# Expert kernel on one core: order of ScalarE's and GpSimd's lists in the experts pass, wider weight pieces, and a key pass in which TensorE turns nothing

## The reference

```
h  = x + layernorm(rs * (attention(layernorm(x) Wq, ctx Wk, ctx Wv) Wo + bo)) * gamma + beta
n  = layernorm(h)                                  # 4096 rows
scores = softmax(n @ gate_weight.T)                # 64 experts
topk_w, topk_idx = top_k(scores, 8), weights normalised to sum 1
for each chosen pair (row, expert e):
    y[row] += w * ((silu(n @ w_gate[e]) * (n @ w_up[e])) @ w_down[e])   # inner width 384
out = h + y
```

## Time and profile before

| | |
|---|---|
| median of 3 runs | 6712.06 us (6709.46 to 6721.78) |
| profiled execution: its own time | 6714.65 us |
| its span, first to last instruction | 6713.0 us |
| granted TensorE clock, mean | 0.983 |
| projections | 12.4 to 1089 us |
| attention and output passes | to 2836 us |
| experts pass, TensorE | 2852.5 to 6695.6 us, 286 tiles |
| busy: PE, DVE, ACT, POOL | 6472.6, 3663.3, 2923.7, 2308.0 us |

### The profile page before, as it was taken

The page is one execution under the profiler, slowest core; times in us unless marked ns, Lnnn a source line. Parts: engine busy times, 40 slices in busy tenths (PEclk is TensorE's granted clock), DMA queues, the critical chain, the costliest instruction groups (busy, mean ns, idle before and its releaser), DMA issues.

```text
span 6713.0 us, 107844 instructions
## 1 busy us (share of the span) xinstructions
PE 6472.6 (96%) x32234; PEld 5731.1 (85%) x32235; DVE 3663.3 (55%) x4544; ACT 2923.7 (44%) x3606; POOL 2308.0 (34%) x2178
## 2 busy tenths in 40 slices
PE   9999999999999999699999999999999999999998
PEld 7888887887888788589989888899899999989987
DVE  4443324999999799744454454443533444444444
ACT  3321224888888655333343343332422333333333
POOL 1000000000000155544545454554444444545554
PEclk9999999999999999899999999999999999999999
DMA  8863555555555676456676676665655656666666
GB/s 258 232 196 143 155 146 144 127 128 127 128 132 130 174 173 171 110 152 160 163 212 162 164 188 160 163 164 111 186 111 111 139 137 164 146 155 164 161 158 149
DMA packets 873577, 1049.72 MB, mean 156 GB/s; under 512 B 440705, under 2 KB 670849, under 8 KB 873474
## 3 DMA queue, kind: packets, MB, share of 16 engines
q0 software_dynamic: 123984, 368.70, 24.0%
q1 hardware_dynamic: 593104, 382.50, 23.6%
q10 hardware_dynamic: 156386, 297.29, 13.2%
HBM read 725.85 MB, written 322.31 MB: 156 GB/s over the span
## 4 chain that ended last, share of the span: by engine, by line
PE 33%; DMA 8%; issue 6%; DVE 4%; POOL 3%; ACT 2%; ACTq 1%; SPq 0%; another core or an unknown queue 0%; POOLq 0%; DVEq 0%
DMA out<-moe_y,moe_rec_s 4%; PE moe_ps_gate L1374 4%; PE moe_ps_gate L1375 4%; PE moe_ps_gate L1376 4%; PE moe_ps_up L1376 4%; PE moe_ps_up L1374 4%; PE moe_ps_up L1375 4%; PE moe_ps_y L1363 3%; PE moe_ps_y L1362 3%; PE moe_ps_y L1361 3%; DMA moe_tokens<-h2st,moe_rows 3%; POOL moe_tokens L1325 2%; DVE moe_ps_turned L1477 1%; DVE moe_d_lo L1467 1%; DVE moe_gu_lo L1467 1%
## 5 line engine op out<-in xcount | busy, mean ns | idle before, releaser
L1325 POOL DMA_INDIRECT moe_tokens<-h2st,moe_rows x1156 | 1273.1, 1101 | 515.2 <-issue 265.7
L1374 PE MATMUL moe_ps_gate<-moe_gu_hi,moe_xT_hi 128*128 128x384 f32 x2288 | 811.3, 355 | 73.8 <-DVE moe_xT_lo L1471 53.9
L1414 ACT COPY moe_y<-moe_ps_y 128x1024 f32<-128x1024 f32 x287 | 291.2, 1015 | 1249.4 <-DMA out<-moe_y,moe_rec_s 1051.9
L1375 PE MATMUL moe_ps_gate<-moe_gu_lo,moe_xT_hi 128*128 128x384 f32 x2288 | 784.4, 343 | 0.0
L1376 PE MATMUL moe_ps_gate<-moe_gu_hi,moe_xT_lo 128*128 128x384 f32 x2288 | 783.4, 342 | 0.0
L1376 PE MATMUL moe_ps_up<-moe_gu_hi,moe_xT_lo 128*128 128x384 f32 x2288 | 764.3, 334 | 0.0
L1375 PE MATMUL moe_ps_up<-moe_gu_lo,moe_xT_hi 128*128 128x384 f32 x2288 | 764.2, 334 | 0.0
L1374 PE MATMUL moe_ps_up<-moe_gu_hi,moe_xT_hi 128*128 128x384 f32 x2288 | 764.2, 334 | 0.0
L1484 DVE SCALAR_TENSOR_TENSOR moe_hidden<-moe_silu,moe_rec_w,moe_ps_up 128x384 f32<-128x384 f32 x286 | 175.8, 615 | 1009.2 <-PE moe_ps_up L1376 694.4
L1361 PE MATMUL moe_ps_y<-moe_d_hi,moe_hT_hi 128*128 128x512 f32 x1722 | 673.5, 391 | 12.8 <-DVE moe_hT_lo L1491 10.3
L1363 PE MATMUL moe_ps_y<-moe_d_hi,moe_hT_lo 128*128 128x512 f32 x1722 | 677.1, 393 | 0.0
(11 more groups left out here) (202 smaller groups left out, 14047.6 us busy)
## 6 DMA issues: line engine op xcount, KB each, us to landing
first_raw<-in_w_gate ACTq DMA_DIRECT2D x63, 1536.0 KB, 7.7
first_raw<-in_w_up ACTq DMA_DIRECT2D x63, 1536.0 KB
moe_raw_d<-in_w_down ACTq DMA_DIRECT2D x63, 1536.0 KB
proj_a_raw<-in_ctxT POOLq DMA_DIRECT2D x64, 512.0 KB, 5.6
kst<-proj_o SPq DMA_DIRECT2D x256, 128.0 KB, 2.8
vst<-proj_o SPq DMA_DIRECT2D x64, 512.0 KB, 2.6
qst<-proj_o SPq DMA_DIRECT2D x256, 128.0 KB, 2.2
att_kt<-kst SPq DMA_DIRECT2D x64, 512.0 KB, 3.5
```

The source lines that it names most:

```text
L1325: nc.gpsimd.indirect_dma_start(out=tokens[:, g * (H // G):(g + 1) * (H // G)], out_offset=None, in_=h2_quarters, in_offset=bass.IndirectOf ...
L1374: nc.tensor.matmul(o[:, 0:I], xT_hi[:, c], gu_hi[:, b, k, c], start=(c == 0), stop=False)
L1375: nc.tensor.matmul(o[:, 0:I], xT_hi[:, c], gu_lo[:, b, k, c], start=False, stop=False)
```

## The change

In the projections pass the transposes by TensorE go, with `tps`, `xT`, their copies and the identity. SyncE stores the normalised rows `xn` as rows (`xnst`), with columns regrouped by quarter; for Q, GpSimd loads a block with four DMAs into `xg`, which reuses the space of `xin` and `xn`, VectorE turns it in four pieces with 32x32 transposes into `a_raw`, and the splits read and write it in the turned order. In the experts pass GpSimd's scatter comes ahead of its gathers, ScalarE's silu is made at the end of the tile before, gate and up are split in 4 pieces (128x1536), some of them placed between other steps, and the load of down moves from the end of an expert to the first tile of the next. TensorE still turns `hidden`.

```diff
+        xin, xn = rows[:, 0:2], rows[:, 2:4]
+        xg = rows[:].rearrange("p q n -> p (q n)").rearrange("p (g n) -> p g n", g=GROUPS)
...
+                    if p == Q:
+                        if not is_first(t2, b):
+                            pool.wait_ge(turned_done, PIECES * t)
+                        for k in range(P // W):
+                            part = xnst[bass.ds(t * HALF, HALF), k * (H * W // P):(k + 1) * (H * W // P)]
+                            pool.dma_start(xg[k * W:(k + 1) * W], part.rearrange("(g b) n -> b g n", b=W)).then_inc(xg_in, 16)
+                        return
...
+                def turn(p, t2, b, k):
+                    n = number(p, t2, b)
+                    dve.wait_ge(xg_in, 16 * (P // W) * (2 * t2 + b + 1))
+                    dve.wait_ge(a_lo_done, (n - 1) * PIECES + k + 1)
+                    columns_of_piece = slice(k * CP * W, (k + 1) * CP * W)
+                    nc.vector.transpose(a_raw[:, chunks(k)].rearrange("p c t -> p (c t)"), xg[:, :, columns_of_piece]).then_inc(turned_done, 1)
...
-                            for c in range(C):
-                                last = nc.tensor.transpose(tps[:, jb, c], xn[:, jb, c * P:(c + 1) * P], ident[:])
-                            last.then_inc(t_done, 1)
...
+        CHUNKS = C // 2
+        GU = 2 * C // CHUNKS
...
                 with pool.Fori(0, last_tile + 1) as t:
+                    add(t - 1)
                     gather(t + 3)
-                    add(t - 1)
...
-                def load_gate_up(e):
-                    act.wait_ge(w_lo_done, PIECES * (e - 1) + GU)
+                def load_gate_up(e, k):
+                    act.wait_ge(w_lo_done, PIECES * (e - 1) + (k + 1) * GU // 2)
...
+                def tile(t):
+                    tokens_high(t + 1)
+                    output(t - 1)
+                    turned_high(t)
+                    gated(t + 1)
+
+                def first_tile(t, e, b, more, is_first):
+                    tokens_high(t + 1)
+                    load_down(e)
+                    split(e, b, 0, 2)
+                    output(t - 1, is_first)
+                    split(e, b, 2, 3)
+                    turned_high(t)
+                    split(e, b, 3, GU)
+                    gated(t + 1)
                     if more:
-                        load_gate_up(e + 1)
+                        load_gate_up(e + 1, 0)
+                        load_gate_up(e + 1, 1)
...
                         split(e + 1, 1 - b, GU, PIECES)
-                        if has_second:
-                            load_down(e + 2)
...
                     tokens_low(t + 1)
+                    if e is not None:
+                        split(e, b, 0, 1)
                     turn_tokens(t + 2)
                     if e is not None:
-                        split(e, b, 0, GU)
+                        split(e, b, 1, 2)
+                    if e is not None:
+                        split(e, b, 2, 3)
                     dve.wait_ge(hT_hi_done, t + 1)
                     nc.vector.tensor_tensor(hT_lo[:], hT_ps, f32(hT_hi[:]), ALU.subtract).then_inc(hT_lo_done, 1)
+                    if e is not None:
+                        split(e, b, 3, GU)
```

More of the change, by code:

```diff
@@ L146, in stores_before @@
         def stores_before(p, t2, b, g):
-            return 16 * (sum(STORES[i] * NB * G // 2 for i in range(p)) + STORES[p] * ((2 * t2 + b) * (G // 2) + g // 2))
+            return 16 * (sum(STORES[i] * NB * ROUNDS // 2 for i in range(p)) + STORES[p] * ((2 * t2 + b) * (ROUNDS // 2) + g // 2))
         def piece(p, half, k):
@@ L163, in norm_tile, with turned, split @@
             return LN * (2 * t2 + b) + g // 2 if g % 2 == 0 else None
-        def transposed_tile(p, t2, b, g):
-            if g % 2 == 0 or p == Q or p == V and not (is_first(t2, b) and g == 1) or p == K and is_first(t2, b) and g == 1:
-                return None
-            if p == V:
-                return LN * NB - 1
-            return LN * (2 * t2 + b) + (g - 3) // 2
-        def stored_tiles(p, t2, b, g):
-            return LN // 2 * (NB if p == V else 2 * t2 + b) + (g - 3) // 2 // 2
+        def turned(p, k):
+            raw = a_raw[:, chunks(k)]
+            if p < Q:
+                return raw
+            return raw.rearrange("p c t -> p (c t)").rearrange("p (g c b) -> p c g b", g=GROUPS, b=W)
+        def split(p, tile, b, k):
+            piece = tile[:, b, chunks(k)]
+            if p < Q:
+                return piece
+            return piece.rearrange("p c (g b) -> p c g b", b=W)
         def chunks(k):
@@ L298, in root @@
                     nc.scalar.activation(std[:, jb], mv[:, jb, 1:2], ACT.Sqrt, bias=eps[:]).then_inc(std_done, 1)
-                def transposed(j, jb, tiles_before):
-                    act.wait_ge(t_done, j + 1)
-                    if not (known(tiles_before) and tiles_before == 0):
-                        act.wait_ge(xT_stored[jb], 16 * tiles_before)
-                    nc.scalar.copy(xT[:, jb], tps[:, jb]).then_inc(xT_done, 1)
                 for k in range(PIECES):
@@ L316, in body @@
                         weights_high(p, 1, 1)
-                    for g in range(G):
+                    for g in range(ROUNDS):
                         evacuate(p, t2, b, g)
@@ L386, in body @@
                         weights_low(p, 1, 1)
-                    for g in range(G):
+                    for g in range(ROUNDS):
+                        if after and after[0] == Q and g < PIECES:
+                            turn(*after, g)
                         evacuate(p, t2, b, g)
@@ L403, in body @@
                     n = number(p, t2, b)
-                    for g in range(G):
+                    for g in range(ROUNDS):
                         if not (p == K and is_first(t2, b) and g < BANKS):
-                            pe.wait_ge(o_lo_done, n * G + g - BANKS + 1)
+                            pe.wait_ge(o_lo_done, n * ROUNDS + g - BANKS + 1)
                         half, r = g // LN, g % LN
@@ L1371, in tile @@
                         for c in range(C):
-                            if e is not None and c % 2 == 0:
-                                pe.wait_ge(w_lo_done, PIECES * e + k * (C // 2) + c // 2 + 1)
+                            if e is not None and c % CHUNKS == 0:
+                                pe.wait_ge(w_lo_done, PIECES * e + (k * C + c) // CHUNKS + 1)
                             nc.tensor.matmul(o[:, 0:I], xT_hi[:, c], gu_hi[:, b, k, c], start=(c == 0), stop=False)
@@ L1426, in load_down, with gated @@
                     act.dma_start(raw_d[:], w_down[bass.ds(e, 1)].rearrange("o (c p) i -> p (o c) i", p=P)).then_inc(raw_in[2], 16)
-                def tile(t, e=None, b=None, more=False, is_first=False):
+                def gated(t):
                     act.wait_ge(gu_done, 2 * t + 1)
```

114 lines of the change are left out of this document (49 added, 65 removed).

## The result

The changed kernel takes 6838.17 us (median of 4 runs, 6830.48 to 6849.09) against 6711.95 for the kernel before: ratio 1.0186, 95% interval 1.0169 to 1.0204. It is 126 us slower, where 149 us less was predicted.

The account below looks back on a forecast made before the run. TensorE was taken as the bound, busy nearly all the time. Gains of 115 us in the experts pass, 29 in the key pass and 4.7 at the end, 149 off 6714.65, gave 6566, as median 6563 us; range 6520 to 6640.

Parts of the forecast that it names:

- Scatter ahead: Experts pass: scatter issued 5.4 us after up's product ends (U), landing before the next `y` needs it; cost 0.
- The cover is 3 us and more even with weights: Experts pass: later gathers still leave VectorE 3 us or more to turn tokens and make `hT_lo`; cost 0.
- Silu last: Experts pass, ScalarE: silu ahead of the down pieces, so no stall at an expert switch, with 0.7 us of cover.
- The 26 stalls: Experts pass: TensorE's waits for `hidden` and the tokens' low part, 4.6 us each; 21 at ordinary switches give 96 us.
- Pieces: Experts pass, VectorE: four wide pieces take 6.8 us, eight narrow about 7.0; the 0.2 us is off TensorE's path.
- One-tile experts: Experts pass: six experts with a single tile, 33 us of stalls after the change against 36 today; gain 3 us.
- the start: Start of the experts pass: two wide pieces instead of eight narrow ahead of `hT_lo`; gain 3.5 us.
- the tenths: Experts pass: 34 us of small losses in many periods without named cause; a third, 12 us, gained.
- Key pass: Projections: TensorE no longer turns 32 tiles at 0.91 us each; gain 29.0 us, lower end 24.
- The end: End of the experts pass: scatter of the last tile but one issued at 6690.3, everything after 4.7 us sooner.
- C: Experts pass: gathers become the bound, period 13.8 instead of 12.80, 286 us more, about 6850 us; chance 0.05.
- the waits of `moe_y` for the scatter near 0: Sign in the profile after that would show the prediction right: `y` copies hardly wait for the scatter.

Follow-up runs that it names:

- e2: The changed kernel with GpSimd's gathers ahead of its scatter again: 6735.09 us, ratio 1.0052 to the kernel before.
- e7: The changed kernel with the scatter's row numbers copied out, so SyncE loads the next record after that copy instead of the landing: 6806.44 us, ratio 1.0157.
- e11: e7 with SyncE loading the scatter's record a whole tile ahead: 6647.33 us, ratio 0.9905.
- e14: e9 with the scatter ahead of the gathers and its record loaded a tile ahead: 6903.23 us, ratio 1.0304.
- e3: The kernel before with only the scatter moved ahead of the gathers: 6883.19 us, ratio 1.0271.
- e8: e4 with the load of down moved into an expert's first tile: 6666.74 us, ratio 0.9954.
- e9: The changed kernel's projections pass with the experts pass of e8: 6659.80 us, ratio 0.9918.
- e4: The kernel before with only the silu moved to the end of ScalarE's list: 6783.95 us, ratio 1.0125.
- e12: e9 with four wide weight pieces in place of eight narrow ones: 6715.84 us, ratio 1.0007.
- e17: e11 with eight narrow weight pieces in the places of the four wide ones: 6626.34 us, ratio 0.9872.
- e16: e11 with `hT_hi` and `hT_lo` ahead of the third wide piece on ScalarE and VectorE: 6625.36 us, ratio 0.9869.
- e1: The kernel before with only the changed projections pass, its experts pass untouched: 6668.37 us, ratio 0.9954.
- e10: e5 with the loads of gate and up held until all four pieces are split: 6757.45 us, ratio 1.0076.
- e5: e2 with the turn ahead of VectorE's first weight piece: 6689.87 us, ratio 0.9986.
- e15: e14 with the load of gate let go once the gate pieces are split: 6901.69 us, ratio 1.0301.

## Why the prediction was wrong

*Scatter ahead* is the step that failed, in two places. The first: "It is issued when `y` is ready: U+5.4". The scatter needs three things: `y`, the landing of the one before, and its own row numbers. The prediction followed the first two. The third comes through SyncE, whose list is ordered for gathers ahead: there `rows_done` comes early in the tile, and the group records are fetched while `rec_s` waits for the scatter's landing anyhow. With the scatter ahead, `rows_done` comes behind it, and the record of the next scatter behind `rows_done`. The profile of before showed the cover: SyncE waited for `hidden` and for the scatter, and 19.9 us only for row numbers. Priced at 0, scatter ahead cost 90 us in the changed kernel (e2). e7 and e11 show that this is the record: moved a tile ahead it takes 169 us off e7 and 189 off after.

The second: "The cover is 3 us and more even with weights; cost 0". These 3 us are U+25.5 less the latest landing, U+20.6, less the turn and `hT_lo`. In a first tile two pieces, 3.4 us, stand between these two, so with weights on the way there was no cover. The paragraph on *Pieces* says as much (a turn beyond U+7.5 eats it), and U+20.6 less a period is U+7.8. The runs have U+8.3 with the scatter in time (e11, e14), and `hT_lo` is late there: 53.0 us of waits in e11, 229 us in e14 with eight pieces behind the turn. By its trace most of the 182 us of e3 is of this kind too. GpSimd's times were too early by 0.9 us for the scatter and 2.7 for the last gather, even in e11.

*Silu last* did what was said of it where it was made: PE's waits for `hidden` are 0 and for `xT_lo` 1.7. But 96 us were booked for it, and it is worth 31 alone (e8) and 24 on top of the key pass (e9). The 26 stalls of the earlier trace rows had two causes in series, the silu behind the down pieces and the `y` behind a late scatter. Taking away one left the other, at `hT_lo`. The prediction relied on *Scatter ahead* to remove that one. That the load of down must move with it, the prediction said in passing; e4 prices it at 115 us (1.0125 against 0.9954).

*Pieces.* Booked as nothing but order. In first tiles the turn was to run from U+5.7 to U+7.0, with the warning that one later than U+7.5 eats the cover. It comes at U+10.2, so `hT_lo` is ready near U+15.3, and the warning is what happened. The width was put at -0.2 us a switch; it costs 60 us in e12, 22 in e17. What makes the wide piece dear was not isolated.

*One-tile experts, the start, the tenths* weren't tested by themselves. The wait for weight pieces grew from 13.4 to 37.8 us where 3 us of gain stood; in e16 it is still 25.3.

*Key pass.* 29.0 predicted, 29.3 in the trace and 31 in e1: this step was right. The starts of K's blocks are 43.52 us apart now. The Trainium skill ("TensorE: Matmul & The Clock Gate", "Back-to-back issue gap") would have had 21 us, by about 81 ns for a sustained matmul of 128 columns; the trace doesn't agree (0.109 us a start before, 29.3 us gone after), and the row of before was the better price.

*The end.* From the last `hT` to the end of the span it is 20.8 us, 23.8 before: 3.0 us of the 4.7.

*The rivals.* C came nearest: it had gathers as the bound and 6850 us, at a chance of 0.05. That the time is near is luck. Its sign of the turn waiting is in the trace, but its mechanism isn't: its ring of turn, gathers and landing would lengthen every period, and the median one is unchanged. The ring that closed runs over SyncE and is longest at a switch of expert. The sign that the prediction asked for, "the waits of `moe_y` for the scatter near 0", failed at first sight (603.5 us after), and holds in e11.

By ratios the way from before to after is: key pass -31, silu last with down -24 (e9), wide pieces +60 (e12), orders +46 (e10), early gate load -60 (e5), piece ahead of the turn +44 (e2), scatter ahead +90: together +125 of 126. The sum closes because each run is the last with one edit more, not because the terms are independent: e11, e15 and e17 show that several change size or sign once the scatter is in time.

## What to carry to other kernels

When an operation is moved ahead in one engine's list, list everything it waits for, small index loads too, and look in the queue that issues them for what stands ahead of each: a ring that was covered by another wait closes when that wait goes. Book a stall to a cure only after asking which second cause would hold the same place; here one third of the booked gain came. Orders of several engines are one design: the pieces placed between other steps lost 46 and 44 us with the gathers ahead (e10, e2), and their absence lost 288 us with the scatter ahead (e15 against e17). When an operation is to come later, add up what stands behind it in its worst tile, not in the ordinary one.

## What the runs showed of the hardware

A scatter that adds 128 rows of 4 KB to memory lands 6.3 us after its issue in tiles without weight loads (medians of 6.3 to 6.4 in all kernels where `y` waits for it). In first tiles, where a switch's loads run, it is 9.2 in the kernel before, 9.4 in e9, e10 and e12, 8.8 in e5, 8.2 in e2 and 10.9 after; the prediction used 6.3 everywhere. The Trainium skill ("DMA: Bandwidth & Descriptors", "Queues, rings and completion order") says that a DMA's semaphore write lands only after every earlier write of the same DMA engine, across its queues. The longer landings among loads would fit that, but no run tells it from mere sharing of bandwidth.

A record of a few bytes a row is not cheap in SyncE's list: with its register loads, `rec_w` to `rec_s` takes 1.4 us, the four group records 2.7, and the loop's counts at a switch, up to the issue of `rec_w`, 2.8 (4142.09 to 4144.90). The landing took 1.7 and 2.5 us in the two places of the ring, and 5.4 in the one before (issued at 4116.13). So the ring is 11.5 us in the ordinary tile shown and 15.7 at the switch.
